# One decoder layer on one core: the loop's last turn written out, VectorE steps cut finer, and the attention passes and the ending in another order

## What is computed

```python
x = _layernorm(x + _L0_attn_ref(x, Wqkv, bqkv, Wo, bo))
# attention: scores = triu(k q^T / sqrt(32)) with -10000 below; softmax; @ v; @ Wo + bo
x = _layernorm(x + _L0_xattn_ref(x, fside, ctx))
def _smooth_quant_linear(x, w):                 # used twice by _L0_xattn_ref, silu(gate) * up between
    s = jnp.sqrt(jnp.maximum(amax_x, EPS) / jnp.maximum(amax_w, EPS))     # by column
    xs, ws = x / s, w * s
    x_scale = jnp.maximum(jnp.max(jnp.abs(xs), axis=-1, keepdims=True), EPS) / QMAX
    w_scale = ...                                                         # the same of ws
    return clip(round(xs / x_scale)) @ clip(round(ws / w_scale)).T * x_scale * w_scale.T
x = _layernorm(x + _L0_ffn_ref(x, gate_w, expert_bias, w1, w2, w3, sw1, sw2, sw3))
# y = sum over the 4 chosen experts of cw * (silu(x w1) * (x w3)) w2; z = (silu(x sw1) * (x sw3)) sw2
```

## Time and profile before

| | us |
|---|---|
| median of 3 runs | 1462.03 (1461.29 to 1467.82) |
| the profiled execution | 1463.37, its span 1461.6 |
| PE busy | 1321.4 (90% of the span), its weight loads 987.2 (68%) |
| DVE, ACT, POOL busy | 868.3 (59%), 438.7 (30%), 403.0 (28%) |
| first pass, until its last `wo` is read | 0 to 147 |
| loop turns 1, 2, 3 | 147 to 298.5, to 454.8, to 608.2 |
| ending with 16 shared halves | to about 768 |
| rest of the shared expert | to about 880 |
| routed tiles, last norm | to 1430, to 1461.6 |

### The profile page before, as it was taken

One profiled execution on the slowest core, in us unless ns is written; L12 is line 12 of the kernel. 1 busy time (PEld: TensorE's weight loads), 2 busy tenths in 40 slices (PEclk: granted clock), 3 DMA queues, 4 the chain that ended last, 5 costly groups with the idle time before them and its releaser, 6 DMA issues.

```text
span 1461.6 us, 24662 instructions
## 1 busy us (share of the span) xinstructions
PE 1321.4 (90%) x7379; PEld 987.2 (68%) x7379; DVE 868.3 (59%) x1455; ACT 438.7 (30%) x651; POOL 403.0 (28%) x495
## 2 busy tenths in 40 slices
PE   7998899989998999779989998999999999879991
PEld 3553455435544555368868887999999998768890
DVE  2452878587658875887658875334433445465534
ACT  1132243414341344222221012223322334353423
POOL 1131013200240024000102842334443443233442
PEclk9899999999899999989999999999999999989995
DMA  8341524242522543404011004545454466668447
GB/s 286 104 117 44 158 81 110 73 129 73 144 73 79 123 114 106 145 15 148 30 58 44 30 30 142 113 76 135 90 129 87 93 161 150 183 178 234 75 75 252
DMA packets 90107, 163.96 MB, mean 112 GB/s; under 512 B 8544, under 2 KB 29536, under 8 KB 89968
## 3 DMA queue, kind: packets, MB, share of 16 engines
q1 hardware_dynamic: 73168, 122.88, 27.6%
q0 software_dynamic: 16816, 39.59, 14.6%
HBM read 113.42 MB, written 49.02 MB: 111 GB/s over the span
## 4 chain that ended last, share of the span: by engine, by line
PE 66%; DVE 16%; DMA 6%; issue 5%; ACT 3%; SPq 1%; DVEq 1%; POOL 1%; ACTq 0%; POOLq 0%
PE psUA L1023 12%; PE psUB L1023 12%; PE psR L1123 10%; PE psY L1030 8%; PE psR L1030 5%; PE psR L1212 3%; PE psOT L1243 3%; PE psTX L1006 2%; PE psST L1226 2%; PE psTH L1039 2%; DMA room<-in_L_ffn_w_dram 2%; DVE xs L1540 1%; PE psR L1137 1%; DVE nm L1622 1%; DVE xs L1528 1%
## 5 line engine op out<-in xcount | busy, mean ns | idle before, releaser
L1023 PE MATMUL psUA<-w_s,xgT 128*128 (+1 forms) x1284 | 241.9, 338 | 7.1 <-DVE xgT L1419 5.2
L1023 PE MATMUL psUB<-w_s,xgT 128*128 (+1 forms) x1284 | 224.7, 323 | 0.0
L1023 PEld LDWEIGHTS psUA<-w_s,xgT 128*128 128x128 f32 x1284 | 212.8, 195 | 13.3 <-DVE xgT L1419 5.3
L1023 PEld LDWEIGHTS psUB<-w_s,xgT 128*128 128x128 f32 x1284 | 210.4, 189 | 0.0
L838 POOL DMA_INDIRECT sx_d<-yg,dst_i x74 | 119.8, 1619 | 302.8 <-ACT yg L916 267.0
L878 ACT ACTIVATE silg<-psUA 128x352 f32<-128x352 f32 x107 | 49.5, 462 | 409.1 <-PE psUB L1023 409.1
L1030 PE MATMUL psY<-w_s,hgT 128*128 (+3 forms) x621 | 162.4, 406 | 0.0
L1428 DVE SCALAR_TENSOR_TENSOR hg<-silg,cws,psUB 128x352 f32<-128x352 f32 x75 | 43.5, 579 | 174.1 <-ACT silg L878 174.1
L800 POOL TENSOR_SCALAR_AFFINE_SELECT pT<-pT 128x128 f32<-128x128 f32 (+1 forms) x192 | 62.1, 342 | 298.8 <-ACT pT L956 298.7
L1622 DVE TENSOR_REDUCE nm<-psR 128x1 f32<-128x128 f32 (+3 forms) x256 | 113.1, 486 | 44.4 <-PE psR L1214 40.5
L1030 PEld LDWEIGHTS psY<-w_s,hgT 128*128 128x128 f32 (+1 forms) x621 | 113.8, 191 | 22.0
(11 more groups left out here) (231 smaller groups left out, 1943.7 us busy)
## 6 DMA issues: line engine op xcount, KB each, us to landing
room<-in_L_ffn_w_dram SPq DMA_DIRECT2D x32, 704.0 KB
scr_d<-qhl SPq DMA_DIRECT2D x32, 512.0 KB, 3.8
qst<-scr_d SPq DMA_DIRECT2D x48, 256.0 KB, 4.1
kst<-scr_d SPq DMA_DIRECT2D x48, 256.0 KB, 6.2
room<-in_L_ffn_w_dram SPq DMA_DIRECT2D x16, 512.0 KB
xt<-in_x_dram SPq DMA_DIRECT2D x5, 1024.0 KB, 7.3
xr<-in_x_dram SPq DMA_DIRECT2D x4, 1024.0 KB, 5.2
breg<-in_fside_BxS2xS_dram SPq DMA_DIRECT2D x4, 1024.0 KB, 8.0
```

What stands on the lines that cost most here:

```text
L1023: mm = pe.matmul(t[:, 0:F], xgT[:, par, a_, c * P:(c + 1) * P], w[:, buf, b_, c, :], start=(c == 0 and n == 0), stop=(c == C - 1 and n == ...
```

## The change

It has four parts, all in the lists and in how VectorE's part of a word is cut; the numbers computed are the same.

1. The loop runs two turns (`Fori(1, B - 1)`). The third is written out as `peel_pass` with the list `PEEL`: that is `SEQ` with a few words more. `raw` behind `ln2` fetches the raw weights of shared half 0 and, after a wait for GpSimd's bias adds, token tiles 0 and 1. `high:0` behind `bc:3` and `high:1` behind `wo:0` split w1 and w3. `lead` stands behind `wo:1`. The fetch of an x that nobody needs (the batch after the last) is gone.
2. Finer steps: `ln1` becomes `wfold:0`, `stat:0`, `ln1`, `xfold`; `ln2` becomes `stat:1`, `ln2`; `s` becomes `s`, `wfold:1`, `sr`; `ws` and `xs` lose their row maxima to `wtop` and `xtop`; `a2` becomes `a2` (ScalarE) and `gate` (VectorE). GpSimd's power now hangs on `stat`.
3. `SEQ` is in a new order. A pass has five fills instead of six, and none among the transposes at its start.
4. `ending` is in a new order, without the splits of w1 and w3 of half 0 and without `lead`, with eight fills instead of nine.

Four fills went, and the transposes of `x2t` stand in two parts between shared work. The diff, cut:

```diff
@@ -148,9 +148,10 @@
+    return ([("wtr", n), ("xtr", n), ("s", n)] + [("wfold", 1)] * (n == 0) + [("sr", n)]
+            + [("ws", n), ("wtop", n), ("wq", n), ("wb", n)] + [("wqt", n, c) for c in range(cn)]
+            + [("xs", n), ("xtop", n), ("xq", n)] + [("xqt", n, c) for c in range(cn)]
+            + [("h", n, i) for i in range(ST)])
@@ -168,21 +169,22 @@
-    "xt:0 xt:1 fill:1 xt:2 xt:3 fill:2 ln1 qk:0 wtr:0 qk:1 xtr:0 s:0 v:0 ws:0 qk:2 wq:0 v:1 qk:3 wb:0 max:0 "
...
-    "lgt route:0 route:1 wo:0 route:2 wo:1 wo:2 route:3 wo:3 ").split()]
+    "xt:0 wfold:0 xt:1 xt:2 stat:0 xt:3 ln1 qk:0 qk:1 xfold v:0 wtr:0 xtr:0 s:0 wfold:1 sr:0 qk:2 ws:0 wtop:0 "
+    "qk:3 wq:0 v:1 v:2 max:0 wb:0 fill:4 max:1 wqt:0:0 max:2 wqt:0:1 wqt:0:2 fill:0 max:3 wqt:0:3 xs:0 xtop:0 "
+    "rows:0 qk:4 v:3 scores:0 xq:0 qk:5 xqt:0:0 xqt:0:1 max:4 fill:2 xqt:0:2 xqt:0:3 scores:1 max:5 h:0:0 "
...
+    "wo:2 wo:3 ").split()]
@@ -261,24 +263,34 @@
+def behind(steps, **more):
+    return [y for x in steps for y in (x, *(step(w) for w in more.get("_".join(map(str, x)), "").split()))]
+late = SEQ.index(("bc", ST - 1))
+PEEL = behind([x for n, x in enumerate(SEQ) if x[0] != "fill" or n < late], ln2="raw", bc_3="high:0", wo_0="high:1", wo_1="lead")
+peel_pass = Pass(PEEL, both_pass.end(B - 2))
...
-    "split:0 lead fill:0 fill:1 fill:2 ln1 ha:0:0 hb:0:0 wtr:0 split:1 xtr:0 s:0 fill:3 fill:4 ha:0:1 hb:0:1 "
...
+    "split:0 wfold:0 stat:0 ha:0:0 ln1 xfold split:1 hb:0:0 fill:0 wtr:0 fill:1 fill:2 fill:3 xtr:0 fill:4 s:0 "
...
+    "h:1:3 hb:5:0 stat:1 ha:5:1 hb:5:1 ln2 ha:6:0 x2t:0 x2t:1 hb:6:0 x2t:2 x2t:3 ha:6:1 lg hb:6:1 lgt route:0 "
+    "route:1 ha:7:0 hb:7:0 route:2 ha:7:1 route:3 hb:7:1 ").split()]
...
-last_pass = Pass(ending, both_pass.end(B - 1))
+last_pass = Pass(ending, peel_pass.end())
...
-    with eng.Fori(1, B) as i:
+    with eng.Fori(1, B - 1) as i:
...
+    walk(peel_pass.steps, B - 1, B - 2, At(peel_pass, None))
@@ -662,10 +674,14 @@
-            At(both_pass, B - 2).let_go(sp, ("qk", 2 * C - 1))
-            shared_expert(0)
...
-            if x == ("xt", C - 1):
+            if x == ("raw",):
+                at.let_go(sp, ("qk", 2 * C - 1))
+                shared_expert(0)
+                sp.wait_ge(s_xrb, ST * B)
+                load_x(0)
+                load_x(1)
+            elif x == ("xt", C - 1) and steps is not PEEL:
@@ -696,8 +712,6 @@
-                load_x(0)
-                load_x(1)
@@ -782,7 +796,7 @@
-            if x[0] in ("ln1", "ln2"):
+            if x[0] == "stat":
@@ -968,8 +982,11 @@
+            elif x[0] == "high":
+                act.wait_ge(s_pv, B * HEADS // 2)
+                split(0, 0, UP[x[1]:x[1] + 1])
...
-                split(x[1], x[1], UP + DOWN)
+                split(x[1], x[1], UP + DOWN if x[1] else DOWN)
@@ -1142,10 +1159,11 @@
+                pe.wait_ge(s_exp, 2 * HEADS * B)
@@ -1494,11 +1511,7 @@
-        def power():
-            asked[0] += 1
-            dve.wait_ge(s_pow, 4 * b + asked[0])
-        def normalise(r, signal, meanwhile=None):
+        def statistics(r):
@@ -1507,9 +1520,8 @@
-            if meanwhile:
-                meanwhile()
-            power()
+        def normalise(r, signal):
@@ -1522,13 +1534,16 @@
-        def scaled(dst, src, t, m, sc, rc):
+        def scaled(dst, src, t):
...
-            dve.wait_ge(s_dfree, at.freed(x) + 1)
-            made(dve.tensor_reduce(m[:, :], dst, AX.X, ALU.max, apply_absolute_value=True))
+        def scales(src, m, sc, rc):
+            dve.wait_ge(s_dfree, at.freed(x))
+            made(dve.tensor_reduce(m[:, :], src, AX.X, ALU.max, apply_absolute_value=True))
@@ -1596,13 +1611,15 @@
+            elif kind == "high":
+                split(0, 0, UP[n:n + 1])
...
-                split(n, n, UP + DOWN)
+                split(n, n, UP + DOWN if n else DOWN)
@@ -1635,10 +1652,23 @@
+            elif kind == "wfold":
+                dve.wait_ge(s_dfree, at.freed(x))
+                if n == 0:
+                    dve.wait_ge(s_bw, 32 * b + 32)
+                largest(wm, wc if n else wf, s_wm)
+            elif kind == "stat":
+                if n:
+                    dve.wait_ge(s_res, ST * (b + 1))
+                else:
+                    dve.wait_ge(s_dfree, at.value(1, 0))
+                statistics(h1 if n else xr)
...
-                dve.wait_ge(s_dfree, at.freed(x))
-                dve.wait_ge(s_bw, 32 * b + 32)
-                normalise(xr, s_qin, lambda: largest(wm, wf, s_wm))
+                dve.wait_ge(s_pow, 4 * b + 1)
+                normalise(xr, s_qin)
+            elif kind == "xfold":
@@ -1656,21 +1686,24 @@
-                if n == 0:
-                    largest(wm, wc, s_wm)
+            elif kind == "sr":
...
-                scaled(xs[:, :, 0:w], wc[:, :, :] if n else wf[:, :, :], t, amw, wsc, rws).then_inc(s_col, 1)
+                scaled(xs[:, :, 0:w], wc[:, :, :] if n else wf[:, :, :], t)
+            elif kind == "wtop":
+                scales(xs[:, :, 0:w], amw, wsc, rws).then_inc(s_col, 1)
...
-                made(scaled(xs[:, :, 0:w], gate_half if n else x1[:, :, :], t, amx, xsc, rxs))
+                scaled(xs[:, :, 0:w], gate_half if n else x1[:, :, :], t)
+            elif kind == "xtop":
+                made(scales(xs[:, :, 0:w], amx, xsc, rxs))
@@ -1680,16 +1713,13 @@
-            elif kind == "a2":
+            elif kind == "gate":
...
-                dve.wait_ge(s_dfree, at.freed(x))
-                dve.wait_ge(s_res, ST * (b + 1))
-                asked[0] = 3
+                dve.wait_ge(s_pow, 4 * b + 4)
```

20 lines of the change are left out of this document (8 added, 12 removed), and 21 rows, old and new, of tables (SEQ, ending).

## The result

The changed kernel takes 1456.6 us (median of 20 runs, 1450.8 to 1462.3) against 1462.6 for the kernel before (20 runs). The ratio is 0.9959, 95% interval 0.9944 to 0.9974: a gain of 6 us, where 22 were forecast. The profiled execution took 1456.8 us with a span of 1454.7.

A forecast was written before the change was run, and what follows sets the result against it. PE was taken to set the time, through idle time and half-clock stretches. Terms of 4.1, 4.2, 3.7, 5.2 and 10.9 gave 28.1 us; less 6 for new waits, 22 us off gave 1440, range 1429 to 1454.

The forecast's parts named there:

- What bounds the kernel: Whole kernel: PE sets the time; its idle time, each with its own releaser, and half-clock stretches can be had.
- First pass: First pass: two PE waits go, 2.9 and 1.5 us, clock gives 1.5, cold start costs 1.8; 4.1 us gained.
- the term for the clock: First pass, 20 us from 40 on at 0.78 clock: 1.5 us won back, bounds 0 and 4.4.
- Start of a turn: From last addition to `scores:0` and `xqt`: finer VectorE steps gain 2.8, 3.9 and 3.8 us in the three turns.
- The rest of a turn: Turn behind its start: waits for an exp and for maxima go, two scores in a row cost 0.8; net 2.2 each.
- Cold starts: Pass starts without fills run at half clock: 1.8 us lost in the first pass, then 0.8, 0 and 0.8.
- The back edge and the exit: Loop jumps: one of two 2.40 us VectorE stops stays, in turn 2; the loop's exit costs nothing.
- The ending: Ending: 3.7 us gained at its start, 3.4 around `x2t`, 3.8 at tile 8; 10.9 us in all.
- Rival (c): Pass starts: without fills each first three products run at 1.2 GHz, making the kernel slower, 1472 us; chance 0.04.
- (d): Ending and turns: fetch blocks ScalarE, DVE's additions end later, turns keep half their gain; 1456 us; chance 0.07.
- The allowance: Whole kernel: 6 us taken off the sum for new waits not worked through, bounds 0 and 12.
- Rival (a): Turns: they give nothing since new waits cancel the old, ending and first pass at half; 1450 us; chance 0.17.

The follow-up runs named there:

- e7: e4 with the first pass alone in its old order; 1449.0 us, ratio 0.9892 to the kernel before.
- e4: The changed kernel with `weigh:2` and `weigh:3` ahead of `scores:4`, and `scores:5` and `scores:6` slightly later; 1445.8 us, ratio 0.9872 to the kernel before.
- e1: The kernel before with only the ending's new order, old passes, three turns in the loop, nothing moved ahead; 1458.0 us, ratio 0.9967.
- e3: The kernel before, both old orders, with only the last pass written out, including its fetches, splits and tile 0; 1459.4 us, ratio 0.9963.
- e5: The changed kernel with SP issuing the six loads of group 2 behind the two small transfers of `rows:1`; 1460.1 us, ratio 0.9976 to the kernel before.
- e9: e6 with the two 8 KB transfers of each `rows:` issued by ScalarE instead of SP; 1456.0 us, ratio 0.9944 to the kernel before.
- e6: e4 with two groups of fills put back between the transposes at the start of a pass; 1439.6 us, ratio 0.9829 to the kernel before.
- e11: The changed kernel with two groups of fills put back between the transposes at the start of a pass; 1451.1 us, ratio 0.9920 to the kernel before.
- e13: e1 without its two groups of fills at the start of a turn; 1455.1 us, ratio 0.9948 to the kernel before.
- e12: e11 with seven groups of fills, 3 us, in front of `scores:4`; 1451.4 us, ratio 0.9934 to the kernel before.
- e14: e6 with two more groups of fills between `weigh:3` and `scores:4`; 1446.8 us, ratio 0.9915 to the kernel before.

## Why the prediction was wrong, point by point

**What bounds the kernel.** PE is busy 90% of the time, and the differences between the experiments lie in its idle time and its clock. That stands. What was wrong is that each idle time could be priced alone: of the moves, those in the ending paid, those in the turns met a wait for something that no PE row of before shows. The clock I had left nearly out of the sum, and by the table it moved further than anything in it.

**First pass: forecast 4.1 us gained, 1.0 lost in the profiled executions, with 3.2 for the new order by e7 against e4.** The wait for `kst` before `max:0` is gone, as said. The wait of 3.99 for `nml` takes its place at 81 us. And the base was misread: the clock of 0.78 of the earlier trace rows is no property of the kernel. In e1 and e3 the same order ran the same stretch like this (windows of e1, then e3):

```profile
40.00:60.00 20.00, 19.80 (x78) 10.93 (x77) 10.63 (x24) 3.28 (x5) 1.91 (x6) 1.00 0.35 81
```

```profile
40.00:60.00 20.00, 20.00 (x58) 10.72 (x58) 8.91 (x18) 0.69 (x1) 0.00 (x0) 0.70 0.33 85
```

with a wait of 2.61 us ahead of it in the one and 3.19 in the other, and first passes of 141.7 and 151.1 us. One profile of before can't tell which is usual; the spread of its three runs, 1461.3 to 1467.8, could have warned me. So the term for the clock, a third of 4.4 us, rests on one execution and is neither borne out nor refuted.

**Start of a turn: forecast 2.8, measured 1.6 in turn 1.** The replay was close. `xfold` ended at 15.5 (15.0), `sr` at 20.1 (19.8), `scores:0` began at 49.4 (48.2) with 0.6 us of wait instead of 1.4. Not foreseen: 1.07 for `xT`, 1.35 instead of 1.0 for the maxima, 1.23 for VectorE's read-out of `v`.

**The rest of a turn: forecast 2.2 gained, measured a loss. This is the step that failed.** "The new list has no fill right behind scores and no such maxima" looked only at whether the old waits go. In turn 1 PE's waits behind `scores:0` are 7.9 us, in the old order 5.0 (e1): 3.10 for `nml`, and 0.78, 0.67, 0.33, 0.79, 0.44, 0.34 and more of small ones. I followed the transfer of the maxima only to `scores:0`, where the queue is empty, with 1.8 us of landing. At `scores:4` the new list has the transfer right behind the six loads in the turns too, and PE there 2.8 us later (1.7 in the first pass): with 1.8 us it would have been no wait of note in the turns, with the 5.8 to 6.1 that it takes it is 3.1 to 3.5. Over the four passes this wait alone is 13.7 us, against an allowance of 6 for all new waits. e4, e5 and e9 show the rest: the landing takes about 6 us behind 1.5 MB on either of the two queues tried, 2.3 ahead of it, and more work ahead of `scores:4` takes 7.9 us of the wait away.

**Cold starts: forecast 0.8 a turn, and 1.8 in the first pass.** 3.4 us in all; e6 and e11 put the fills' worth at 5.5 to 6.2 for the four passes, of which some 2 are the wait for `xT`. The size was roughly right, the place was not: the starts of turn 1 and of the written-out turn ran at full clock (16 products in 7.13 and 7.11 us), where I had put 0.8 each, that of turn 2 did not (14 in 8.38), where I had put nothing, and most of the loss was elsewhere. The rule of the Trainium skill, page "TensorE: Matmul & The Clock Gate", section "Why this matters for your kernels", against idle gaps, which I had turned into 14 us for four starts, points the right way for e6 and the wrong way for e13, which has the gaps and loses nothing by the median. Rival (c) fell.

**The back edge and the exit.** One stop of VectorE remains, at turn 2 (1.75 us in the row below, VectorE after). The written-out turn has none on VectorE, but PE stood 2.28 us at the loop's exit before its first transposes, which I had at nothing:

```profile
304.88 3.67 DVE L1534 TENSOR_REDUCE wm<-breg 128x512 f32<-128x2048 f32 x1 [1.75 <-issue]
```

```profile
458.67 1.96 PE L1154 MATMUL psR<-ident,xt 128*128 128x128 f32 x16 [2.28 <-issue]
```

PE would have waited there for the last addition anyway, to about the same moment. The turn was forecast 5.2 shorter and came out 0.7 shorter, with 2.3 us of splits and tile 0 in it (an estimate of the prediction); it holds 3.11 us of `nml`.

**The ending: forecast 10.9, measured 9.9 with the routed tiles, 7.6 up to them.** The junction went by its replay, with the end of the last addition at 611.2 (610.0) and the up product 20.2 us behind it (20). The product ran at half clock, 1.7 us, which I had not counted. ScalarE waited 0.77 us for the fetch and `lgt` was not late: (d) did not come. The wait for `x2t` is gone. At tile 8 the wait is 1.95 (1.4) and the product 3.19 us (2.18 at full clock):

```profile
754.17 3.19 PE L1040 MATMUL psUA<-w_s,xgT 128*128 128x352 f32 x12 [1.95 <-DVE xgT L1437]
```

Mechanism right, size off by some 3 us up to the routed tiles; 2.7 us of clock at these two products are the part that can be named. e1 and e3 bear it out from the other side: 7.1 and 5.7 (4.8 and 5.4 by the ratios).

**The allowance and the rivals.** The 6 us for "new waits" were put beside the sum, not where they would arise; the measured misses are 5.1, 7.8, 2.9 and 4.4 us in first pass and turns (1.0 in the ending with the routed tiles). Rival (a), "the turns give nothing", was the right one of the four and still 6 us short: they took. Its reason, small new waits in place of the old, is what the idle times of e4 show once the large one is cut. That e6 lands on 1439.6, the forecast's 1440, is chance: its parts are not those of my sum.

## What stays open

What sets the clock's falls. The table gives 24 to 53 us of them for versions that differ in a few fills, and they come at other places in each: e12, e13 and e14 show that filling idle time is no sure way to fewer. Nor is it known why kernels with the new turns run at the higher mean clock, and so whether the 6 us of the change are owed to its order or to that. The profile of e14 has an untouched stretch 4.3 us longer, and all its five runs are longer than those of e6 (1445.1 to 1449.6 against 1439.0 to 1440.4); neither is explained. How much of e9's 16 us is ScalarE's stop and how much clock was not tried apart.

## What to carry to other kernels

When a new order moves a step that a small transfer feeds, write down what its DMA engines carry at that moment, not only what stands ahead of it on its own engine: 1.8 us in the quiet rows of before became 6 behind six large loads, on both queues tried, and of the edits tried only more work ahead of the consumer gained time. The old trace has no row for a wait that its order avoided, but it can hold the landing: here 5.4 us in the first pass of before. So, before pricing moves one by one, set for every such pair the time from issue to consumer in the new order against the landing in the worst place, not the best. And compare kernels by the mean clock of many runs: one execution's clock in one stretch is not a quantity to be won back, and a gain can be all clock.

## What the runs showed of the hardware that I had not expected

An 8 KB transfer issued right behind 1.5 MB of loads landed 5.4 to 6.6 us after its issue on the same queue (before, after, e4, e6) and 5.7 to 6.2 on another engine's queue (e9); issued ahead of them 1.8 to 2.3 us (e5), alone 1.8 (before, turn 1). The granted clock falls at different places in kernels that differ only in a few filling products, with 24 us to 53 us lost by the table's reading, and the same order of the first pass ran one stretch at 1.00 in e1 and at 0.70 in e3. The mean clock of a run goes with the kernel: 0.949 to 0.962 with the old turns, 0.958 to 0.975 with the new.
